# Third layer's bias: rounding and splitting moved to the second tile on 128 partitions, and copied into its two rows within SBUF

## The reference, cut to what matters

```python
router_logits = x @ Wr + br
expert_mask = jax.nn.one_hot(jnp.argmax(router_logits, axis=-1), num_experts, dtype=x.dtype)
for e in range(num_experts):
    h = jax.nn.gelu(x @ W1[e] + b1[e], approximate=False)
    h = jax.nn.gelu(h @ W2[e] + b2[e], approximate=False)
    y = h @ W3[e] + b3[e]
    out = out + expert_mask[:, e:e + 1] * y
```

## Time and profile before

| | |
|---|---|
| median of 3 runs | 791.76 us (791.49 to 793.59) |
| profiled execution, its own time | 792.73 us |
| its span | 791.0 us |
| busy: PE, DVE, ACT, POOL | 716.1, 474.5, 453.0, 433.4 us |
| attention stage, to the end of iteration 15 | up to about 447 us |
| drain of the pipeline, iterations 16 and 17 | about 447 to 473 us |
| routing | about 473.5 to 486 us |
| expert stage | from about 486 us |

### The profile page before, as it was taken

The page is one execution under the profiler, slowest core; times in us unless marked ns, Lnnn a source line. Parts: engine busy times, 40 slices in busy tenths (PEclk is TensorE's granted clock), DMA queues, the critical chain, the costliest instruction groups (busy, mean ns, idle before and its releaser), DMA issues.

```text
span 791.0 us, 26602 instructions
## 1 busy us (share of the span) xinstructions
PE 716.1 (91%) x9191; PEld 608.5 (77%) x9192; DVE 474.5 (60%) x1389; ACT 453.0 (57%) x1070; POOL 433.4 (55%) x566
## 2 busy tenths in 40 slices
PE   4799999999999999999999674999999999997995
PEld 3688788888888888888888573787888788875874
DVE  1455666676667666766677638998952990288000
ACT  2556566666666666666666205656657557563752
POOL 6356555555555555555554411577576776674543
PEclk9899999999999999999999996999999999999998
DMA  5322222322332233333322801229124422271000
GB/s 168 88 80 75 75 74 86 86 73 73 86 86 73 73 86 86 72 74 86 86 73 88 320 28 50 80 85 324 41 94 156 135 100 85 85 243 32 20 7 1
DMA packets 55007, 73.85 MB, mean 93 GB/s; under 512 B 5839, under 2 KB 40688, under 8 KB 54962
## 3 DMA queue, kind: packets, MB, share of 16 engines
q1 hardware_dynamic: 49716, 60.96, 25.8%
q0 software_dynamic: 2944, 8.13, 3.4%
q10 hardware_dynamic: 2304, 4.20, 1.4%
HBM read 66.91 MB, written 7.27 MB: 94 GB/s over the span
## 4 chain that ended last, share of the span: by engine, by line
PE 67%; DVE 10%; issue 10%; POOL 4%; DMA 3%; ACT 3%; SPq 1%; POOLq 1%; DVEq 0%; ACTq 0%
PE ps_s L1459 14%; PE ps_kv L1181 8%; PE ps_p L1220 5%; PE ps_kv L1173 5%; PE ps_o L1206 4%; PE ps_s L1192 4%; PE ps_p L1411 3%; PE ps_o L1479 3%; PE ps_kv L1411 3%; DVE w L1158 3%; DVE w L1155 3%; PE ps_m L1316 2%; PE ps_m L1312 2%; PE ps_m L1270 2%; PE ps_s L1443 2%
## 5 line engine op out<-in xcount | busy, mean ns | idle before, releaser
L725 ACT ACTIVATE prob<-prob,neg_max 128x257 f32<-128x257 f32 x256 | 112.8, 501 | 68.6 <-DVE neg_max L912 68.5
L912 DVE CUSTOM_DVE_ANT_0 prob<-ps_s,mask_add 128x257 f32<-128x257 f32 x256 | 95.5, 420 | 50.7 <-PE ps_s L1192 50.5
L1155 DVE CAST w<-w_raw 128x512 fp32r<-128x512 f32 (+1 forms) x108 | 68.2, 632 | 66.8 <-DMA w_raw<-in_L_ffn_W_dram 60.4
L1158 DVE TENSOR_TENSOR w<-w_raw,w 128x512 fp32r<-128x512 f32 (+1 forms) x128 | 102.8, 803 | 5.1 <-DVE w L1158 0.9
L1459 PE MATMUL ps_s<-w,h_hi 128*128 x368 | 93.9, 406 | 12.5 <-DVEq L1161 7.0
L568 POOL TENSOR_TENSOR ctx_parts<-ctx_raw,ctx_parts 128x512 fp32r<-128x512 f32 x64 | 82.3, 1286 | 37.6 <-ACT ctx_parts L720 37.4
L1173 PE MATMUL ps_kv<-ctx_parts,wkv_hi 128*128 128x256 f32 x512 | 86.7, 297 | 10.3 <-DVE wkv_hi L1025 10.3
L1459 PEld LDWEIGHTS ps_s<-w,h_hi 128*128 128x128 f32 x368 | 68.6, 190 | 32.4 <-issue 17.8
L1181 PE MATMUL ps_kv<-wkv_hi,ctx_parts 128*128 128x256 f32 x512 | 87.1, 299 | 2.7 <-ACT kT L729 0.3
L1220 PE MATMUL ps_p<-ident,prob 128*128 128x128 f32 x512 | 80.1, 277 | 0.9 <-DVE probT L934 0.8
L1173 PEld LDWEIGHTS ps_kv<-ctx_parts,wkv_hi 128*128 128x128 f32 x512 | 71.4, 191 | 11.7 <-issue 10.3
(11 more groups left out here) (198 smaller groups left out, 1523.9 us busy)
## 6 DMA issues: line engine op xcount, KB each, us to landing
w_raw<-in_L_ffn_W_dram SPq DMA_DIRECT2D x24, 1024.0 KB, 7.9
ctx_raw<-in_ctx_turned_dram SPq DMA_DIRECT2D x64, 256.0 KB, 3.4
mask_add<-mask_dram SPq DMA_DIRECT2D x64, 128.5 KB, 3.3
rows_dram<-x3n ACTq DMA_DIRECT2D x16, 256.0 KB, 3.7
w_raw<-in_L_ffn_W_dram SPq DMA_DIRECT2D x8, 512.0 KB
xt<-in_x_dram SPq DMA_DIRECT2D x16, 128.0 KB, 2.6
xr<-in_x_dram SPq DMA_DIRECT2D x16, 128.0 KB, 2.3
slot_x<-rows_dram,slot_ids POOLq DMA_INDIRECT x23, 3.7
```

The source lines that it names most:

```text
L725: a.activation(prob[:, g, :], prob[:, g, :], ACT.Exp, bias=neg_max[:, g:g + 1], scale=-1.0).then_inc(exp_done, 1)
L912: d.tensor_tensor_reduce(prob[:, r, :], ps_s[r][:, 0:J], mask_add[:, k, :], -(HD ** -0.5), 3.0e38, ALU.add, ALU.min, neg_max[:, r:r + 1]). ...
L1155: d.tensor_copy(w[:, b, HI, part], raw[:, b, part]).then_inc(rounded, 1)
L1158: d.tensor_tensor(w[:, b, LO, part], raw[:, b, part], f32(w[:, b, HI, part]), ALU.subtract).then_inc(rounded, 1)
```

## The change

The load of b3 brings it in once, as 128 partitions of 16 columns (`b3_cols`), where it had been two rows of 2048. POOL rounds and splits it in this form at the end of iteration 1, right after the two fills, into `b3_col_parts` (two parts of 128 x 16). SP, after `ahead(2)` and ahead of its loop, waits for `b3_split` and issues two transfers within SBUF, each of which writes one part into its row of `b3_parts` (`b3_placed`). The three operations at the end of iteration 15 are gone, and so is DVE's wait in the expert stage; PE waits for `b3_placed` instead of `b3_split`. The two new tiles take 64 and 128 bytes of a partition.

```diff
-        b3_raw = over("b3_raw", "area", place23(1, HI), [P, E * D])
+        b3_cols = sb("b3_cols", [P, E * D // P])
+        b3_col_parts = sb("b3_col_parts", [P, 2, E * D // P], F32R)
...
-            for row in (0, 32):
-                sp.dma_start(b3_raw[row:row + 1, :], b3.rearrange("(o e) d -> o (e d)", o=1)).then_inc(b3_in, 16)
+            sp.dma_start(b3_cols[:, :], b3.rearrange("e d -> (e d)").rearrange("(p n) -> p n", p=P)).then_inc(b3_in, 16)
             ahead(2)
+            sp.wait_ge(b3_split, 1)
+            for part, row in ((HI, 0), (LO, 32)):
+                sp.dma_start(b3_parts[row:row + 1, :].rearrange("o (p n) -> o p n", p=P).bitcast(F32),
+                             b3_col_parts[:, part, :].bitcast(F32)).then_inc(b3_placed, 16)
             with sp.Fori(3, TILES) as T:
                 ahead(T)
...
                     g.memset(ones_r[:, :].bitcast(F32), 1.0).then_inc(b3_zeroed, 1)
-                if isinstance(T, int) and T == TILES - 1:
                     pool.wait_ge(b3_zeroed, 2)
-                    pool.wait_ge(b3_in, 32)
-                    pool.wait_ge(last_prob_kept, B)
-                    for row in (0, 32):
-                        g.tensor_copy(b3_parts[row:row + 1, :], b3_raw[row:row + 1, :]).then_inc(b3_rounded, 1)
-                    pool.wait_ge(b3_rounded, 2)
-                    g.tensor_tensor(b3_parts[32:33, :], b3_raw[32:33, :], b3_parts[32:33, :].bitcast(F32), ALU.subtract).then_inc(b3_split, 1)
-                    pool.wait_ge(b3_split, 1)
+                    pool.wait_ge(b3_in, 16)
+                    g.tensor_copy(b3_col_parts[:, HI, :], b3_cols[:, :]).then_inc(b3_rounded, 1)
+                    pool.wait_ge(b3_rounded, 1)
+                    g.tensor_tensor(b3_col_parts[:, LO, :], b3_cols[:, :], b3_col_parts[:, HI, :].bitcast(F32), ALU.subtract).then_inc(b3_split, 1)
...
-                    if not first_matrix and e == 1 and n == 0:
-                        dve.wait_ge(b3_split, 1)
...
-            pe.wait_ge(b3_split, 1)
+            pe.wait_ge(b3_placed, 32)
```

More of the change, by code:

```diff
@@ L239, in perceiver_kernel @@
         b3_split = sem("b3_split")
+        b3_placed = sem("b3_placed")
         early_rounded = sem("early_rounded")
```

## The result

The changed kernel takes 797.54 us (median of 8 runs, 795.40 to 799.14). The kernel before, run beside it, takes 793.84 us (median of 8, 791.49 to 795.22). The ratio is 1.0051, 95% interval 1.0033 to 1.0068: about 4.0 us slower, between 2.6 and 5.4. I had forecast 794.0 us, which was a loss of 2.25 us on a median of 791.76 us, and a range up to 797.5. The direction is one to which I had given the same chance as to no change; the size is short by 0.4 to 3.2 us, and the median lies just outside the range. Two things make that miss, and the experiments separate them: the base on which the sum was put, and one term of the sum.

What follows compares the result with a forecast made beforehand. PE, busy for 716 of 791 us, was taken to bound the kernel. A loss of 7.9 us at the seam less a gain of 5.65 gave +2.25 on the median of 791.76: 794.0 us, range 790.3 to 797.5.

Steps and rivals of the forecast that it cites:

- The standstill at the seam: Between iterations 1 and 2, SP's wait delays the load of xt, making the fourth score operation 5.7 us late.
- The low clock behind it: After PE's standstill between iterations 1 and 2, its clock restarts low, costing 2.2 us, bounded by 0 and 3.4.
- Seam in all: Between iterations 1 and 2, the late score and the low clock together lose 7.9 us, range 5 to 10.
- `attnT`: At iteration 15's end, this DVE operation, freed from waiting for POOL's subtraction, takes 0.43 us, saving 3.93.
- After only 0.7 us without work, and I expect the clock to stay up: At iteration 15's end, PE restarts early at full clock, so three chain pieces take 2.49 us, not 4.21.
- the 5.65: Gain in us at iteration 15's end, from a shorter attnT and a full PE clock; x3n starts earlier by this.
- my own lower bound of 3.5 us: Gain at iteration 15's end if the clock falls all the same and attnT takes 0.81 us.
- The base: Whole kernel: the sum of +2.25 us was applied to the median before the change, 791.76 us.
- No fall of the clock at the seam: Rival, between iterations 1 and 2: standstill without a low clock, total 791.8 us; chance 0.18.
- Made up in the loop: Rival, iterations 2 to 14: the seam's delay is regained, down to 786.1 us if all; chance 0.07.
- No gain at `attnT`: Rival, iteration 15's end: attnT is long for another reason, such as weight loads; 799.7 us; chance 0.05.
- Slow transfers: Rival, ahead of SP's loop: the transfers within SBUF issue slowly or hold up xt; 796 to 797 us; chance 0.10.

Runs made afterwards that it cites:

- before_wait: The kernel before with only a wait by SP for POOL's two fills added between ahead(2) and its loop: 799.15 us, ratio 1.0066 to the kernel before.
- xt_first: The changed kernel with ahead(3) written out and SP's wait and two transfers directly behind tile 3's xt load: 792.78 us, ratio 0.9973 to the kernel before.
- padded: peeled with 58 idle transposes in TensorE's standstill at the start of iteration 2: 795.64 us, ratio 1.0000 to the kernel before.
- late_read: late with two one-row fills and a subtraction reading SBUF, all useless, on POOL at iteration 15's end: 795.75 us, ratio 0.9997 to the kernel before.
- late_write: late with four useless POOL fills of 128 rows, which only write, at iteration 15's end: 792.21 us, ratio 0.9955 to the kernel before.
- late_2: late run once more, unchanged, as a control: 790.29 us, ratio 0.9956 to the kernel before.
- again: The changed kernel run once more, unchanged: 798.57 us, ratio 1.0038 to the kernel before.
- late: The changed kernel with SP's wait and its two transfers moved behind SP's loop: 791.47 us, ratio 0.9969 to the kernel before.
- peeled: The changed kernel with TensorE's iteration 2 written out instead of being first in its loop: 798.04 us, ratio 1.0019 to the kernel before.
- all_late: The changed kernel with all b3 work at iteration 15's end, SP's wait and transfers behind its first weight loads: 789.70 us, ratio 0.9939 to the kernel before.
- late_thin: late with 6 idle transposes before and 6 behind the last prob transposes in iteration 15: 790.83 us, ratio 0.9965 to the kernel before.
- all_late_pads: all_late with late_thin's transposes and more in iteration 17 and ahead of the expert stage: 787.95 us, ratio 0.9927 to the kernel before.

## Why the prediction was right and wrong

- **The standstill at the seam: right.** Forecast: `b3_split` at 79.65, `xt` issued at 80.95, 5.7 us late at the fourth score. Measured, with the 0.58 us added: 79.6, 81.2, 5.28. The transfers took longer to issue than taken (1.19, not 0.90), and `xt` landed sooner behind them: DVE began 2.01 us after the issue, not 2.8. POOL's small operations start 0.28 us apart (78.27, 78.55, 78.83); the 0.3 that I took was right, though the earlier trace rows, which I gave for it, show 0.18. before_wait and xt_first show the cause from both sides.
- **The low clock behind it: right in kind, a little smaller.** Forecast 2.2, measured 1.80 and 1.44 (the stretch to Wo, 6.52 and 6.16 against 4.72). In the profile of padded it is absent. Seam in all: 7.08 and 6.78 us against 7.9.
- **`attnT`: right.** 0.43 us, as taken; late_read and late_write show the cause.
- **"After only 0.7 us without work, and I expect the clock to stay up": this step failed.** It put 1.7 us of the 5.65 on the clock. From Wo in iteration 2 to `top`, the changed kernel gains 3.01 us and 3.29 in its second profile. I had looked only at the one long standstill and not at PE's short waits ahead of it. They were there before (0.79, 0.72 us) and sit in the changed kernel too (0.79, 1.03); PE is busy for less than half of 449.2 to 452.6, and then the clock falls. That it can stay up, late_2 shows, and there the gain is 5.47. Of the 2.46 us between late_2 and the changed kernel 0.70 lie ahead of Wo in iteration 16 and 1.76 behind it. Of the profiles without the long standstill and without added transposes at this place the clock fell in six (the change, again, late, xt_first, peeled, padded) and stayed up in three (late_2, late_write, all_late). That the short waits bring it down is not shown: in late_2 PE is hardly busier in the matching stretch (the window below), and the clock stays up; so it did in the kernel before (1.81 us busy from 442.3 to 445.7, clock 1.00).

```profile
444.20:447.60 3.40, 1.81 (x12) 1.33 (x12) 1.05 (x5) 0.65 (x3) 0.76 (x2) 1.00 1.02 407
```

The term was an "if", and I took it as certain; my own lower bound of 3.5 us would have been the better value. With it the sum is 7.9 - 3.5 = 4.4 us, with the measured terms (means of the two profiles) 6.9 - 3.15 = 3.8, near the measured 4.0 and 3.0. That the whole sum missed by only 1.5 us is in part luck: the seam was 0.8 to 1.1 us smaller than forecast, and this made up for a part of the 2.4 to 2.6 us that the gain lacks.
- **What is left of the profiles' difference.** The two spans differ by 5.2 us: -0.58 ahead of the seam, +7.08 at it, -3.01 to `top`, +0.40 to layer 2, and +1.3 in the rest of the expert stage. That last part was 290.2 us in the profile of before and 290.6 to 291.7 in late, late_2, all_late, before_wait and again, with or without the wait. Over all the profiles it runs from 290.2 (before, late_thin) to 294.7 (all_late_pads), so nothing here speaks for an effect of the change; the profile of before was a short one there.
- **The base.** The median of the three runs shown was 791.76; all 91 runs of the kernel before in this study have a median of 794.3, from 791.4 to 799.6. 2.1 us of the distance between 794.0 and 797.54 came from there (793.84 beside it), and only 1.5 from the sum. The 0.97 us by which the profiled execution lay above the median was a hint that three runs didn't hold the spread.
- **The rivals.** No fall of the clock at the seam: it fell in both profiles. Made up in the loop: not; the delay at Wo in iteration 2 was 6.50 us, and at the product of `turned` with `lqk` at the end of iteration 15 (L1320 before, L1319 after) it was 6.36 (it starts at 442.38 before and 448.74 after). No gain at `attnT`: refuted. Slow transfers: 1.19 us for both, no hold-up of `xt`.

Not settled is how often each fall of the clock comes, and what decides it. The intervals of single kernels are 3 to 5 us wide, and one or two profiles of each show different patterns.

## What to carry to other kernels

A wait put into a load queue costs what the next load behind it is late for: read which load that is, when it was issued, and how long its user already waited, since with no slack one position in the queue decides the sign. A long GpSimd operation that reads SBUF can hold a VectorE operation with two inputs there (`attnT`, 4.36 us against 0.43), so the cost of such an operation is looked for in the neighbour's durations, not in its own engine's waits. And a gain that rests on TensorE's clock staying up is written as two cases, since the same program had it both ways here.

## What the runs showed of the hardware that I had not expected

The clock fell behind a stretch without any long standstill: PE was busy for 1.58 of 3.40 us and then ran at 0.51 for 3.35 us. The same program in the same place ran once wholly at 0.50 and once at 1.00. Behind a wait of PE of 2.2 us the clock was low in five profiles of six. A POOL fill of one row took as long as one of 128 rows (1.79 and 1.80 us for 2048 columns), so it is the shorter row in each partition that made the split short: 3 operations in 8.3 us on one row of 2048, 2 in 0.5 us as 128 x 16. And two transfers of 8 KB within SBUF, into one row each, took SP 1.19 us to issue, while the load of `xt` behind them, with 128 rows, took 0.35.
